# Two more groups of the gated FFN made with seven block products, and z of the later batches kept in memory as parts

## The reference, cut to what matters

```python
x = x + attention(cond(x, f, ...), Wq, Wk, Wv, Wo, betas)     # 16 heads, segments of 128 tokens
z = cond2(x, f, f, w, u, cond_512)                            # below
up_gate = einsum('bsd,hd->bsh', z, W1)                        # B=4, S=512, D=512, H=2048
up_lin = einsum('bsd,hd->bsh', z, W3)
hidden = fwht(silu(up_gate) * up_lin)                         # fast Hadamard transform along H
out = x + einsum('bsh,dh->bsd', hidden, W2)
# cond2: a <- a * decay + exp(k) * v and b <- b * decay + exp(k) along the tokens, forward and backward,
# z = sigmoid(x) * (num / max(den, 1e-8)) * (0.8 + 0.2 * tf)
```

## Time and profile before

| what | value |
|---|---|
| median of 3 runs | 1578.29 us (1578.01 to 1578.4) |
| the profiled execution, its own time | 1582.11 us |
| its span, first to last instruction | 1580.3 us |
| mean granted TensorE clock | 0.948 |
| TensorE matmuls | 1544.1 us busy (98%), 8406 |
| VectorE | 1227.1 us busy (78%) |
| ScalarE | 780.9 us (49%) |
| GpSimd | 614.9 us (39%) |

### The profile page before, as it was taken

The page is one execution under the profiler, slowest core; times in us unless marked ns, Lnnn a source line. Parts: engine busy times, 40 slices in busy tenths (PEclk is TensorE's granted clock), DMA queues, the critical chain, the costliest instruction groups (busy, mean ns, idle before and its releaser), DMA issues.

```text
span 1580.3 us, 24552 instructions
## 1 busy us (share of the span) xinstructions
PE 1544.1 (98%) x8406; PEld 1326.8 (84%) x8406; DVE 1227.1 (78%) x2746; ACT 780.9 (49%) x1687; POOL 614.9 (39%) x433
## 2 busy tenths in 40 slices
PE   4899999999999999999999999999999999999999
PEld 2688988888888888888888888888888888888887
DVE  8879968898888788888765764666897888677785
ACT  3566656545625526544555562663554443444442
POOL 3656657252111212222001010144664466666662
PEclk9899999999999999999999999999999999999999
DMA  5366677586584486386288558247211222311111
GB/s 176 119 226 240 236 264 275 190 317 251 187 309 158 155 313 238 105 296 222 78 295 313 201 210 334 93 162 258 87 54 54 64 88 69 107 49 59 54 41 54
DMA packets 113405, 276.58 MB, mean 175 GB/s; under 512 B 11648, under 2 KB 36608, under 8 KB 111872
## 3 DMA queue, kind: packets, MB, share of 16 engines
q1 hardware_dynamic: 94416, 241.96, 42.4%
q10 hardware_dynamic: 18864, 33.04, 6.7%
HBM read 226.71 MB, written 48.25 MB: 174 GB/s over the span
## 4 chain that ended last, share of the span: by engine, by line
PE 91%; DVE 5%; issue 2%; ACT 1%; POOL 0%; DMA 0%; ACTq 0%; SPq 0%; DVEq 0%; POOLq 0%
PE psG L666 14%; PE psG L668 14%; PE psG L667 14%; PE psG L790 6%; PE psX L862 4%; PE psX L666 3%; PE psX L668 3%; PE psX L667 3%; PE psX L817 3%; PE psG L792 3%; PE psZ L843 3%; PE psZ L834 3%; PE psZ L842 2%; PE psZ L668 2%; PE psY L668 2%
## 5 line engine op out<-in xcount | busy, mean ns | idle before, releaser
L2226 POOL TENSOR_TENSOR parts<-stage,parts 128x512 fp32r<-128x512 f32 x160 | 235.6, 1494 | 136.5 <-ACT parts L1717 134.2
L666 PE MATMUL psG<-yh,parts 128*128 128x512 f32 x646 | 263.3, 408 | 0.1
L668 PE MATMUL psG<-yh,parts 128*128 128x512 f32 x646 | 253.1, 392 | 0.0
L667 PE MATMUL psG<-yl,parts 128*128 128x512 f32 x646 | 252.2, 390 | 0.0
L2294 POOL TENSOR_TENSOR vs<-v,omb 128x512 f32<-128x512 f32 x64 | 92.9, 1475 | 391.6 <-PE psX L817 214.6
L668 PEld LDWEIGHTS psG<-yh,parts 128*128 128x128 f32 x646 | 121.3, 188 | 26.6
L666 PEld LDWEIGHTS psG<-yh,parts 128*128 128x128 f32 x646 | 121.9, 189 | 22.1 <-issue 0.9
L667 PEld LDWEIGHTS psG<-yl,parts 128*128 128x128 f32 x646 | 122.0, 189 | 21.3
L790 PE MATMUL psG<-heads,parts 128*128 128x512 f32 x384 | 135.5, 395 | 0.0
L1717 ACT ACTIVATE parts<-stage 128x512 fp32r<-128x512 f32 x152 | 87.8, 622 | 50.8 <-DMA stage<-in_w 15.7
L1875 ACT ACTIVATE kT<-psG 128x512 f32<-128x512 f32 x62 | 36.9, 595 | 151.5 <-PE psG L668 150.1
(11 more groups left out here) (281 smaller groups left out, 4151.8 us busy)
## 6 DMA issues: line engine op xcount, KB each, us to landing
parts<-high_o SPq DMA_DIRECT2D x52, 512.0 KB, 6.2
parts<-low_o SPq DMA_DIRECT2D x52, 512.0 KB, 7.6
parts<-high_v SPq DMA_DIRECT2D x36, 512.0 KB, 5.1
parts<-low_v SPq DMA_DIRECT2D x36, 512.0 KB, 6.5
stage<-in_w SPq DMA_DIRECT2D x64, 256.0 KB, 3.1
parts<-high_k SPq DMA_DIRECT2D x23, 512.0 KB, 5.5
parts<-low_k SPq DMA_DIRECT2D x23, 512.0 KB, 7.2
parts<-high_q SPq DMA_DIRECT2D x23, 512.0 KB, 4.6
```

Source lines behind the costliest of these rows:

```text
L666: e.matmul(out, lh, rh, start=first, stop=False, skip_group_check=check)
L667: e.matmul(out, lh, rl, start=False, stop=False, skip_group_check=check)
L668: return e.matmul(out, ll, rh, start=False, stop=last, skip_group_check=check)
L2226: e.tensor_tensor(lo, raw, hi, ALU.subtract).then_inc(p_wl, 1)
```

## The change

Groups 6 and 7 are made with seven products too (`FASTS` in place of `FAST`, `FAST0` = 6). Since groups 6 and 7 belong to the first half, the half's own T sums are needed, for batches 0 and 1; their raw z is not kept, so `t_part` adds high and low parts first and `t_sum` works on that. The parts of T of the first half are put in the room of zh2, zl2, zh3, zl3. So z of batches 2 and 3 has to be finished before group 6: `shared_out_ffn` spreads the same steps over units 0 to 9, with the rooms 2500, 2500, 2900, 2900. It is then written to memory as high and low parts (`z_out`, four DMAs of 1 MB, `late_s`) and fetched back during the end of group 7 (`z_back`). Raw late z is no longer kept, so the second half's T sums begin with `t_part` as well. On the engines `plain_unit` now holds the code of a plain unit, used for units 1 to 11, and, between groups 7 and 9, for 16 and 17 (`late_ups` on TensorE).

```diff
@@ -124,16 +124,21 @@
 UPTO, DONE = shared_out()
 
 
+FAST0 = 6
+FASTS = list(range(FAST0, NG)) + list(range(NG + 1, 2 * NG))
+FAST_NO = {g: i for i, g in enumerate(FASTS)}
 LATE = (("zsig", 0), ("zt", 690), ("zh", 0), ("zl", 690), ("zload", 0))
-FSTEPS = [(name, t, cost) for t in range(NA, NT) for name, cost in SCAN + LATE]
-FROOM = (1400, 1400, 1900, 1900)
+LATE_ORDER = list(range(NA, NT))
+LATE_AT = {t: q for q, t in enumerate(LATE_ORDER)}
+FSTEPS = [(name, t, cost) for t in LATE_ORDER for name, cost in (SCAN if t >= NA else ()) + LATE]
+FROOM = (2500, 2500, 2900, 2900)
...
     upto, at, left = {}, 0, 0
-    for u in range(17):
+    for u in range(2 * FAST0 - 2):
...
         T1, T2, T3, T4 = 0, 2, 1, 3
+        room = {T3: zh2, T1: zl2, T2: zh3, T4: zl3}
+        t_hi = [[room[k][:, 0:2, :] for k in range(4)],
+                [yh[k // 2][:, 2 * (k % 2):2 * (k % 2) + 2, :] for k in range(4)]]
+        t_lo = [[room[k][:, 2:4, :] for k in range(4)],
+                [yl[k // 2][:, 2 * (k % 2):2 * (k % 2) + 2, :] for k in range(4)]]
+        late_z = [zh2, zl2, zh3, zl3]
...
@@ -898,11 +932,11 @@
                 i = PLACE[kind, g]
                 hi, lo = ring(i)
                 wait_split(w, i)
-                w.wait_ge(a_zh, 4 * b + 4)
                 if b < 2:
+                    w.wait_ge(a_zh, 4 * b + 4)
                     w.wait_ge(p_zl, 4 * b + 4)
                 else:
-                    w.wait_ge(v_zl, 4 * (b - 2) + 4)
+                    wait_late_z(w, b)
                 for c in range(NC):
                     cols = slice(256 * c + 128 * j, 256 * c + 128 * j + 128)
                     m = three(bank[:, :], hi[:, cols], lo[:, cols], zh[b][:, c, :], zl[b][:, c, :],
...
                     for dc in range(NC):
                         down(u - 1, dc)
+
+            def late_ups(i):
+
+
+                for u in (2 * NG, 2 * NG + 1):
+                    for k, (j, kind) in enumerate(UPS):
+                        if u > 2 * NG:
+                            w.wait_ge(v_f1 if kind == "1" else v_f3, 2 * (u - 1) + j + 1)
+                        elif k == 0:
+                            w.wait_ge(v_f1, 4 * NG - 1)
+                        elif k < 3:
+                            w.wait_ge(v_cc, 6 * i + 4 + k)
+                        else:
+                            w.wait_ge(v_f3, 4 * NG - 1)
+                        up(u, j, kind, bank_of(u, k))
+                    for dc in range(NC):
+                        down(u - 2, dc)
 
             def a_z(bank, kind, g, j, half, zhi, zlo, first, last):
 
...
+            def t_part(place, half):
+
+
+                b, c = {T1: (2 * half, 0), T3: (2 * half + 1, 0), T2: (2 * half + 1, 2), T4: (2 * half, 2)}[place]
+                if half == 0:
+                    w.wait_ge(a_zh, 16)
+                    w.wait_ge(p_zl, 8)
+                    w.wait_ge(v_zl, 8)
+                    w.wait_ge(d_ho, 16 * 8)
+                else:
+                    wait_late_z(w, b)
+                    w.wait_ge(v_f1, 4 * NG)
+                    w.wait_ge(v_f3, 4 * NG)
+                e.tensor_tensor(t_raw[place], zh[b][:, c:c + 2, :].bitcast(F32), zl[b][:, c:c + 2, :].bitcast(F32),
+                                ALU.add).then_inc(v_ts, 1)
+
+            def t_sum(place, other, half, turned=False):
+
+                w.wait_ge(v_ts, 8 * half + {T1: 4, T3: 5, T2: 6, T4: 7}[place])
                 a, b = (t_raw[other], t_raw[place]) if turned else (t_raw[place], t_raw[other])
                 e.tensor_tensor(t_raw[place], a, b, ALU.subtract).then_inc(v_ts, 1)
+
+            def sums_of_z(half):
+
+                for place in (T1, T3, T2, T4):
+                    t_part(place, half)
+                t_sum(T1, T3, half, True)
+                t_sum(T3, T2, half, True)
+                t_sum(T2, T1, half)
+                t_sum(T4, T2, half)
 
             def s_sums(kind, g):
 
...
+            def plain_unit(u, before):
+
+
+                half = u // (2 * NG)
+                sums = u in (2 * FAST0 - 2, 2 * NG)
                 for j in range(2):
-                    if u == 2 * NG and j == 0:
-                        t_sum(T1, T3, True)
-                        t_sum(T3, T2, True)
                     if (u, j) != (1, 0):
                         gate(u, j, "1", bank_of(u, 2 * j))
                         gate(u, j, "3", bank_of(u, 2 * j + 1))
                     behind_ffn(u, j)
-                    if u == 2 * NG and j == 0:
-                        t_sum(T2, T1)
-                        t_sum(T4, T2)
-                        s_sums("1", FAST[0])
-                if u + 1 == 2 * FAST[0]:
-                    break
+                    if sums and j == half:
+                        sums_of_z(half)
+                        s_sums("1", FAST0 if half == 0 else NG + 1)
+                if before is None:
+                    return
                 for dc in range(NC):
-                    add_x(u - 1, dc)
...
+            def high_t(place, half, n):
+
+                w.wait_ge(v_ts, 8 * half + 4 + n)
+                if half == 0:
+                    w.wait_ge(d_zo, 64)
+                else:
+                    w.wait_ge(pe_1, 4 * NG)
+                    w.wait_ge(pe_3, 4 * NG)
+                    w.wait_ge(pe_x, 4 * (NG - FAST0))
+                e.activation(t_hi[half][place], t_raw[place], ACT.Copy).then_inc(a_sw, 1)
 
...
+            def plain_unit(u):
+
+
+                half = u // (2 * NG)
+                g = ffn[u][0]
+                turned = u in (2 * FAST0 - 1, 2 * NG)
+                split_hi(PLACE["2", g] + (3 if u % 2 == 0 or g + 1 in FAST_NO else 4))
                 for j in range(2):
                     if u > 1:
                         sigmoid(u, j, bank_of(u, 2 * j))
                         high_h(u, j)
                     behind_ffn(u, j)
-                    if u == 2 * NG and j == 0:
+                    if turned and j == half:
                         for n, place in enumerate((T1, T3, T2, T4)):
-                            high_t(place, n + 1)
-                        high_s("1", FAST[0])
+                            high_t(place, half, n + 1)
+                        high_s("1", FAST0 if half == 0 else NG + 1)
                 behind_ffn(u, 2)
                 behind_ffn(u, 3)
+
+            for u in range(1, 2 * FAST0):
+                plain_unit(u)
 
             def take(i, g, k, kind, bank, value):
 
...
+            def z_out():
+
+                w.wait_ge(a_zh, 16)
+                w.wait_ge(v_zl, 8)
+                for r in range(4):
+                    e.dma_start(late_s[r], late_z[r][:, :, :].bitcast(F32)).then_inc(d_zo, 16)
+
+            def z_back():
+
+                i = FAST_NO[NG - 1]
+                w.wait_ge(d_zo, 64)
+                w.wait_ge(pe_3, 4 * (NG - 1) + 3)
+                e.dma_start(zl2[:, :, :].bitcast(F32), late_s[1]).then_inc(d_zb, 16)
+                w.wait_ge(pe_x, 4 * i + 3)
+                e.dma_start(zh2[:, :, :].bitcast(F32), late_s[0]).then_inc(d_zb, 16)
+                e.dma_start(zh3[:, :, :].bitcast(F32), late_s[2]).then_inc(d_z, 16)
+                w.wait_ge(pe_3, 4 * (NG - 1) + 4)
+                e.dma_start(zl3[:, :, :].bitcast(F32), late_s[3]).then_inc(d_z, 16)
 
             def behind_ffn(u, k):
                 for name, t, _ in FSTEPS[late[0]:FUPTO.get((u, k), late[0])]:
                     if name == "zload":
-                        load_z(t + 2)
...
+            load_z(0)
             load_w(PLACE["2", 0] + 2)
             load_x(0)
             load_w(PLACE["2", 0] + 3)
             load_x(1)
+            load_z(1)
+
...
@@ -2617,20 +2766,26 @@
                 g, b = ffn[u - 1]
                 if u == 1:
                     load_w(PLACE["2", 0] + 4)
-                elif u % 2 == 0 and g < NG - 1:
-                    load_w(PLACE["3", FAST[0]] + 1 if g == NG - 2 else PLACE["2", g] + 7)
-                elif u % 2 == 0 and g + 2 in FAST:
+                elif u % 2 == 0 and g < FAST0 - 2:
+                    load_w(PLACE["2", g] + 7)
+                elif u % 2 == 0 and g == FAST0 - 2:
+                    z_out()
+                    load_w(PLACE["3", FAST0] + 1)
+                elif u == 2 * NG - 1:
+                    z_back()
+                    load_w(PLACE["3", NG + 1] + 1)
+                    out_of(u - 1)
+                elif u == 2 * NG:
+                    load_w(PLACE["2", NG + 1] + 1)
+                    out_of(u - 1)
+                elif u % 2 == 0 and g + 2 < 2 * NG:
                     load_w(PLACE["3", g + 2] + 1)
-                elif u % 2 == 0 and g + 1 in FAST:
+                elif u % 2 == 0 and g + 1 < 2 * NG:
                     load_w(NW)
                 for k in range(4):
                     behind_ffn(u, k)
-                if g % NG == NG - 1:
-                    for dc in range(NC):
-                        w.wait_ge(v_x, 4 * (u - 1) + dc + 1)
```

(5 more changed lines are left out.)

195 lines of the change are left out of this document (116 added, 79 removed).

## The result

The changed kernel takes 1653.76 us (median of 6 runs, 1653.24 to 1655.08), the kernel before 1578.26 beside it: a ratio of 1.048, 95% interval 1.0469 to 1.0491. It is slower by 75.5 us; the forecast was 1653, with 1608 to 1679 as its range. The profiled execution has a span of 1651.4 us.

A forecast was written before the change was run, and what follows sets the result against it. TensorE was taken as the bound, with VectorE close behind. Matmuls saved -5.4, stall +67.7, clock +1.7 and group 9 +10.3 gave +74.3 us on the 1578.3 median: 1653 us, range 1608 to 1679.

The forecast's parts named there:

- The matmuls saved: Groups 6 and 7: 12 matmuls fewer each at 0.227 us, 5.4 us saved on TensorE, the whole gain.
- VectorE in units 1 to 9: Late steps at 1.22 times plan take 116.0 us, waits 10.9; last zl ends at 1274.6; TensorE stalls every unit.
- The chain: From last zl to group 6's first T1 product: loads behind stores, sums, low parts, 51.8 us; whole stall 67.7.
- third rival: Group 6's weight loads overtake the stores of z, sigmoid ready about 8 us after the zl: 1645 us, 10%.
- The clock: TensorE's granted clock falls after the long idle time before group 6's first T1 product, adding 1.7 us.
- the signs: Profile signs: largest TensorE idle times ahead of unit 11's second up half and first T1 product; about 9 before unit 15's down.
- Ahead of group 9: Unit 14's additions come late, so down of unit 15 stalls: 10.3 us net, bounds 0 and 14 (weight sums also wait).
- The bounds 1635 to 1673: Forecast's own total range from factor 1.16 to 1.34, chain 49 to 56 and group 9 0 to 14.
- the fetch: z_back before unit 16: its first two transfers land 7.5 us after issue, no stall; bounds 0 and 2.
- The plan holds: Rival 1: late steps cost only their planned times, without surcharge or waits; stall 33.3 us, 1608 us, 12%.
- Faster: Rival 2: late steps end before unit 10, the rest fits into unit 10 and unit 11's up: 1573 us, 5%.
- Worse: Rival 4: factor 1.49 throughout and half-clock stalls in every unit, 26 us more on VectorE: 1679 us and above, 5%.

The follow-up runs named there:

- e1: The kernel before with only the table of rooms changed to 2500, 2500, 2900, 2900: 1605.37 us, ratio 1.0172.
- e2: The changed kernel with SyncE issuing the loads of group 6's W1 and W3 ahead of the four stores of z: 1639.71 us, ratio 1.0389.
- e5: The changed kernel with sums of z before unit 16's gates, T's parts after its first hh and hl, weight sums after unit 14's additions: 1642.11 us.
- e3: As e2, with ScalarE and GpSimd making T's high and low parts in unit 10 in place of unit 11: 1638.74 us, ratio 1.0383.
- e4: The changed kernel with each late tile's reciprocals covering 4 of 128 columns: 1643.11 us, ratio 1.0411.
- e9: Orders of e3 and e5 together (1626.92 us), plus late exponentials of slots 2 and 3 put off behind the next unit's first hh: 1636.52 us.
- e11: As e9, with the exponentials put off behind the next unit's second hh in place of its first: 1635.9 us, ratio 1.0364.

## Why the prediction was right

**The whole.** +75.5 us measured, +74.3 forecast. The mechanism stood: VectorE's late steps hold up units 2 to 9, and behind the last `zl` a chain of loads, sums and low parts holds up group 6. The runs split the loss: 27.0 for the rooms (e1), 14.1 for the loads behind the stores (e2), 11.7 for the order ahead of group 9 (e5), less 5.4 for the matmuls (from the trace). What is left, 28.1, is by the traces: 22 of stall between unit 10 and the first T1 product that e2 still has (the sums of z, T's low parts), 2 at the lower clock behind it, and some 4 ahead of group 9. No run leaves out the sums of z or the low parts; that the 22 us are theirs is a reading of the traces, and e3, which moved them, won nothing. The two traces from unit 2 on give the same whole: 62.3 of stall up to the first T1 product, 2.1 at the lower clock, 1.1 ahead of unit 16, 14.5 in units 16 and 17, 1.0 in group 9 (its first `down` waits 0.76 us for an `hh`, which the forecast hadn't), less 5.4.

**The matmuls saved.** 24 instructions less and groups 6 and 7 at 29.9 us each: as forecast.

**VectorE in units 1 to 9.** The last `zl` ends 171.3 us after unit 2's start; the forecast was 175.1. From 1096.0 on VectorE is busy for 157.3 us, 45.6 of them gates and additions, so the late steps took 111.7 and the factor was 1.17, not 1.22; the waits were 13.1, not 10.9. The size was nearly right, but one reason was too simple: "TensorE stalls some 3 us in every unit" was wrong (the idle ahead of `psG` is 3.9 and 4.1 us in units 4 and 9, and 0 in 5 and 10; and 11.2 of the 26.3 us lost there are slower matmuls), and "VectorE has no slack left" only half true. e4 shows the bound to be VectorE and ScalarE in turns, each in its own order.

**The chain.** 50.1 us from the last `zl` to T1, against 51.8: the sigmoid was ready 16.4 us behind the `zl` (16.2), the first T1 product at 221.5 us after unit 2's start (226.9), the stall was 62.3 (67.7). Each link of the chain stood where it was named. TensorE's idle time didn't: its largest piece, 15.11 us, is ahead of unit 11's first `up`, which waits for the same late sigmoid, and the signs had named only the second half of unit 11's `up` (7.52) and the first T1 product (8.68, forecast 12). The third rival's way, loads that overtake stores, didn't occur; its sum comes to 1644, not 1645. The Trainium skill's rule ("DMA: Bandwidth & Descriptors", section "Queues, rings and completion order") allows another order but doesn't promise one; here all four halves landed behind all four stores.

**The clock.** Behind 8.68 us of idle time the granted clock was 0.50 (1.2 GHz) from 1316.5 to 1320.5: the first six matmuls came at a pitch of 0.450 us, the next six at 0.345, then 0.227 again: 2.05 us, against 1.7.

**Ahead of group 9.** This is the term of the sum that was mis-sized: "10.3", measured 15.5 for units 16 and 17, 14.5 net of the old loss, and 1.1 more in front of unit 16 for the fetched parts, where 0 was taken. Gates (16, 1) were done after 19.3 us, not 17, and the additions of unit 14 began after 39.8, not 36, so TensorE's wait ahead of `down` of unit 15 was 13.14, not some 9: two weight sums at GpSimd's pace, 2.56 us each, which the bound of 14 had and the middle value hadn't in full. The working of this term doesn't close either: its parts make 17 + 6.1 + 1.0 + 10.3 = 34.4 where it says about 36, and from 36 the stall is 9.5, not 9.3. (The bounds 1635 to 1673 likewise come to 1634 to 1672 from their terms.)

So the good total is partly luck: the stall was taken 5.4 us too long, this term and the fetch 5.3 too short. By the mechanism alone the forecast was good to some 5 us in each term, not to 1.

**The rivals.** "The plan holds" (1608) is refuted by e1: the plan alone costs 27 us. "Faster" would have needed the last `zl` by 1209.5 on the clock of the trace before, 110.0 after unit 2's start; it came 171.3 after. "Worse" needed a factor of 1.49; it was 1.17.

## What to carry to other kernels

When optional work is moved to an earlier deadline, sum it against the slack of the engine that makes it, and follow each of its waits through the next engine's order: 5.4 us of matmuls saved were paid with 27 us for the pace and 54 for what stood behind the last `zl` and ahead of group 9. Before a queue is given a transfer that waits for late data, look at what stands behind it: the loads ahead of the stores were worth 14 us. And idle time of a helping engine ahead of a step isn't a gain to be had by moving the step; it pays only if what then stands in front of the waited-for step gets shorter (e3, e9 and e11 gained nothing or lost 9).
